# First attention of a two-block kernel: the last chunk's scores are computed a second time and its penalty is subtracted in PSUM

## The reference

```python
scores = jnp.einsum('bthd,bghd->bhtg', Q, K) / np.sqrt(DH)
topv, topi = jax.lax.top_k(scores, K_TOP)          # K_TOP = 32
probs = jax.nn.softmax(topv, axis=-1)
attn = jnp.zeros_like(scores).at[bi, hi, ti, topi].set(probs)
attn_mean = attn.mean(axis=1)                      # over the 4 heads
c_t = jnp.einsum('btg,bgd->btd', attn_mean, V)
```

## Time and profile before

| What | Value |
|---|---|
| Median of 3 executions | 2037.97 us (2029.82 to 2042.62) |
| Profiled execution, its own time | 2042.3 us |
| Its span in the trace | 2040.5 us |
| Mean granted TensorE clock | 0.889 of full speed |
| PE busy | 1603.4 us (79%) |
| ACT busy | 1387.9 us (68%) |
| DVE busy | 914.9 us (45%) |
| POOL busy | 180.9 us (9%) |
| L753 (scores, 832 passes) | 387.5 us |
| L907 (masking products, 128) | 239.3 us |
| L835 (exponentials, 128) | 208.9 us |
| L819 (copies of scores, 224) | 205.8 us |

### The profile page before, as it was taken

How to read it: one execution, slowest core, us unless ns; L and a number is a source line. 1 busy time by engine, 2 the same in 40 slices (tenths; PEclk the granted TensorE clock), 3 DMA queues, 4 the chain that set the end, 5 groups by cost and what they waited for, 6 DMA issues and landing times. The chain is left out here.

```text
span 2040.5 us, 23175 instructions
## 1 busy us (share of the span) xinstructions
PE 1603.4 (79%) x8229; PEld 618.9 (30%) x8229; DVE 914.9 (45%) x2862; ACT 1387.9 (68%) x1382; POOL 180.9 (9%) x153
## 2 busy tenths in 40 slices
PE   5347877879788878358351999999999999996996
PEld 3236334445445445244220111111111111113332
DVE  4733799999999999837131000000000000003323
ACT  3462767777778686520221999999999999993332
POOL 2753010111111111100000000000000000000000
PEclk7566978999998999679665999999999999997998
DMA  2122076776966967747302000430070000003000
GB/s 85 49 90 96 10 154 136 173 174 136 204 148 134 216 135 172 164 113 97 59 3 46 1 1 1 34 35 1 1 64 5 1 1 1 1 1 89 0 0 11
DMA packets 91353, 145.12 MB, mean 71 GB/s; under 512 B 46704, under 2 KB 59465, under 8 KB 90433
## 3 DMA queue, kind: packets, MB, share of 16 engines
q0 software_dynamic: 13472, 75.53, 18.7%
q1 hardware_dynamic: 77328, 67.19, 15.5%
q10 hardware_dynamic: 432, 0.85, 0.1%
HBM read 54.15 MB, written 13.99 MB: 33 GB/s over the span
## 5 line engine op out<-in xcount | busy, mean ns | idle before, releaser
L1735 ACT ACTIVATE ex<-ps 128x1536 f32<-128x1536 f32 x544 | 731.2, 1496 | 1.6 <-PE ps L1694 1.5
L1707 PE MATMUL ps<-ex,V 128*9 128x512 f32 x3264 | 427.6, 596 | 0.2 <-ACT ex L1735 0.2
L753 PE MATMUL ps<-K,qst 128*128 128x512 f32 (+1 forms) x832 | 387.5, 611 | 23.2 <-ACT srow L819 17.4
L1694 PE MATMUL ps<-Q,K 52*128 52x512 bf16 x1632 | 329.2, 385 | 67.5 <-PEq L106 33.7
L947 DVE MAX8 cand<-srow 128x8 f32<-128x128 f32 x1600 | 353.6, 283 | 6.9 <-ACT srow L819 6.5
L1745 DVE COPY o<-ps 9x512 f32<-9x512 f32 x32 | 22.0, 687 | 745.8 <-PE ps L1707 745.0
L819 ACT COPY srow<-ps 128x1024 f32<-128x1024 f32 (+1 forms) x224 | 205.8, 921 | 88.9 <-PE ps L753 88.1
L907 DVE SCALAR_TENSOR_TENSOR both<-srow,top,both 128x1536 f32<-128x1536 f32 (+1 forms) x128 | 239.3, 1870 | 13.1 <-ACT both L835 13.0
L753 PEld LDWEIGHTS ps<-K,qst 128*128 128x128 f32 x832 | 161.3, 205 | 182.2 <-issue 139.7
L835 ACT ACTIVATE both<-srow,shift 128x1536 f32<-128x1536 f32 (+1 forms) x128 | 208.9, 1635 | 7.7 <-DMA both<-both 6.6
L1694 PEld LDWEIGHTS ps<-Q,K 52*128 52x128 bf16 x1632 | 60.3, 94 | 484.8 <-ACT ex L1735 446.7
(11 more groups left out here) (306 smaller groups left out, 1142.2 us busy)
## 6 DMA issues: line engine op xcount, KB each, us to landing
both<-both POOLq DMA_DIRECT2D x69, 768.0 KB, 8.4
v_ring<-v_rows SPq DMA_DIRECT2D x96, 256.0 KB, 3.8
both<-both POOLq DMA_DIRECT2D x23, 898.0 KB, 12.5
K<-k_parts SPq DMA_DIRECT2D x48, 204.0 KB
k_parts<-kl SPq DMA_DIRECT2D x12, 384.0 KB, 2.5
V<-v_rows SPq DMA_DIRECT2D x4, 918.0 KB, 33.3
v_rows<-v1g SPq DMA_DIRECT2D x12, 288.0 KB, 3.0
v_rows<-V SPq DMA_DIRECT2D x12, 256.0 KB, 3.2
```

The source lines that it names most:

```text
L753: last = M.matmul(ps[:, GBANK * (k % RING) + b, 0:c1 - c0], qst[:, h, :], K0[:, c0:c1], start=True, stop=True)
L1694: last = M.matmul(ps[:, n % 6, :], K1[rows_, quad % 2, hh // 2, g * P:(g + 1) * P], Q1[rows_, 4 * quad + hh, tb * TB:(tb + 1) * TB], start ...
L1707: last = M.matmul(ps[32 * j:32 * j + VW, 6 + w % 2, :], V1[:, quad % 2, g, VW * j:VW * j + VW], ex1[:, (4 * g + j) % NSLOT, :], start=g == ...
L1735: C.activation(ex1[:, n % NSLOT:n % NSLOT + NBANK, :], ps[:, n % 6:n % 6 + NBANK, :], ACT.Exp)\
```

## The change

For items 0 to 30 the last chunk (columns 4608 to 6404) goes another way. ScalarE computes `penalty` = Relu(2^100 x (32nd largest - score)) in bf16 from `srow`: zero where the score is kept, very large elsewhere. TensorE computes the chunk's scores a second time into two more ring places (1024 and 772 columns, `AGAIN`) and adds to each, in the same PSUM accumulation, a bf16 product of `minus` (the negated identity) and `penalty`. ScalarE takes the exponential straight from that PSUM (`exps_again`), which gives zero where the penalty is large. VectorE's masking product of that chunk is gone; it computes one more column, `steep` = 2^100 x 32nd largest. The ring's places get a common numbering (`RING_AT`), the queries are placed two items ahead rather than four, VectorE's three other masks move to pieces 41, 45 and 49, and GpSimd's transfer for the last chunk of item n - 1 is issued ahead of those of item n. The last item, 31, is treated as before.

```diff
@@ -658,11 +658,21 @@
     CH_OF = [3, 3, 3, 4]
     NCH = len(CH_OF)
     CUTS = [min(4 * P * sum(CH_OF[:c]), G) for c in range(NCH + 1)]
+    LOW = NCH - 1
     LAST = NI - 1
     SLOTS = 3
-
-
-    MASK_AFTER = {38: 0, 42: 1, 46: 2, 49: 3}
+    STEEP = 2.0 ** 100
+
+
+    MASK_AFTER = {41: 0, 45: 1, 49: 2}
+    AGAIN = [(c0, min(c0 + GCOL, G)) for c0 in range(CUTS[LOW], G, GCOL)]
+    RING_AT = {}
+    for n in range(NI + 1):
+        for g in range(NGRP):
+            if n < NI:
+                RING_AT["first", n, g] = len(RING_AT)
+            if n >= 2 and g >= NGRP - len(AGAIN):
+                RING_AT["again", n - 2, g - NGRP + len(AGAIN)] = len(RING_AT)
     NEEDS = {j: c for c in range(NCH) for j in range(sum(CH_OF[:c]), sum(CH_OF[:c + 1]))}
     TURNED_BY = {c: sum(CH_OF[:c + 1]) for c in range(NCH)}
     SPREAD = [3, 5, 7, 9, 11, 13, 15, 17, 19, 21, 23, 24, 25]
@@ -687,6 +697,9 @@
         cand = sb(b2, "cand", [P, 2, LONG])
         top40 = sb(b2, "top40", [P, SLOTS, 40])
         edges = sb(b2, "edges", [P, NI, 3])
+        penalty = sb(b2, "penalty", [P, G - CUTS[LOW]], BF16)
+        minus = sb(b2, "minus", [P, P], BF16)
+        steep = sb(b2, "steep", [P, SLOTS])
         nmax = sb(b2, "nmax", [P, SLOTS])
         zsum = sb(b2, "zsum", [P, SLOTS])
         lnz = sb(b2, "lnz", [P, SLOTS])
@@ -719,7 +732,13 @@
             return (t * (H0 - 1) + h) * 16 * PARTS[c]

         def kept_by(n, c):
-            return n * NCH + c + 1
+            return n * LOW + c + 1
+
+        def evac_by(n, g):
+            return RING_AT["first", n, g] + 1
+
+        def again_by(n, r):
+            return RING_AT["again", n, r] + 1

         STEPS = 10

@@ -743,7 +762,7 @@
             def _(pe):
                 def scores(n, g):
                     t, h = divmod(n, H0)
-                    k = n * NGRP + g
+                    k = RING_AT["first", n, g]
                     if k >= RING:
                         pe.wait_ge(S("evac"), k - RING + 1)
                     pe.wait_ge(S("q_placed"), n + 1)
@@ -752,6 +771,19 @@
                         c0, c1 = g0 + b * 512, min(g0 + b * 512 + 512, g1)
                         last = M.matmul(ps[:, GBANK * (k % RING) + b, 0:c1 - c0], qst[:, h, :], K0[:, c0:c1],
                                         start=True, stop=True)
+                    last.then_inc(S("scored"), 1)
+
+                def scores_again(n, r):
+
+                    k = RING_AT["again", n, r]
+                    pe.wait_ge(S("evac"), k - RING + 1)
+                    pe.wait_ge(S("penalized"), n + 1)
+                    g0, g1 = AGAIN[r]
+                    for b in range(-(-(g1 - g0) // 512)):
+                        c0, c1 = g0 + b * 512, min(g0 + b * 512 + 512, g1)
+                        out = ps[:, GBANK * (k % RING) + b, 0:c1 - c0]
+                        M.matmul(out, qst[:, n % H0, :], K0[:, c0:c1], start=True, stop=False)
+                        last = M.matmul(out, minus[:, :], penalty[:, c0 - CUTS[LOW]:c1 - CUTS[LOW]], start=False, stop=True)
                     last.then_inc(S("scored"), 1)

                 def turn_group(u, j):
@@ -790,13 +822,18 @@
                         if j > 0:
                             value_group(u, j - 1)

-                for n in range(NI):
+                pe.wait_ge(S("minus_ready"), 1)
+                for n in range(NI + 1):
                     for g in range(NGRP):
-                        scores(n, g)
-                        mean_step(n * NGRP + g)
+                        if n < NI:
+                            scores(n, g)
+                        if ("again", n - 2, g - NGRP + len(AGAIN)) in RING_AT:
+                            scores_again(n - 2, g - NGRP + len(AGAIN))
+                        if n < NI:
+                            mean_step(n * NGRP + g)
                 if NI * NGRP - 1 in MEAN_AT:
                     value_group(*MEAN_AT[NI * NGRP - 1])
-                pe.wait_ge(S("evac"), NI * NGRP)
+                pe.wait_ge(S("evac"), len(RING_AT))
                 for j in range(NTURN):
                     turn_group(NT - 1, j)
                     if j > 0:
@@ -813,9 +850,12 @@
                     g0, g1 = group(g)
                     if n >= SLOTS:
                         below = [c for c in range(NCH) if CUTS[c] < g1]
-                        act.wait_ge(S("kept"), kept_by(n - SLOTS, below[-1]))
-                    act.wait_ge(S("scored"), n * NGRP + g + 1)
-                    b = GBANK * ((n * NGRP + g) % RING)
+                        act.wait_ge(S("kept"), kept_by(n - SLOTS, min(below[-1], LOW - 1)))
+                        if below[-1] == LOW:
+                            act.wait_ge(S("penalized"), n - SLOTS + 1)
+                    k = RING_AT["first", n, g]
+                    act.wait_ge(S("scored"), k + 1)
+                    b = GBANK * (k % RING)
                     C.copy(srow[:, n % SLOTS, g0:g1], ps[:, b:b + GBANK, :].rearrange("p a b -> p (a b)")[:, 0:g1 - g0])\
                         .then_inc(S("evac"), 1)

@@ -835,11 +875,28 @@
                     C.activation(both[:, home(n), chunk(c)], srow[:, s, chunk(c)], ACT.Exp, bias=shift[:, s:s + 1])\
                         .then_inc(S("exped"), 1)

+                def penalties(n):
+
+                    s = n % SLOTS
+                    act.wait_ge(S("steep_ready"), n + 1)
+                    C.activation(penalty[:, :], srow[:, s, chunk(LOW)], ACT.Relu, scale=-STEEP, bias=steep[:, s:s + 1])\
+                        .then_inc(S("penalized"), 1)
+
+                def exps_again(n, r):
+
+                    s, k = n % SLOTS, RING_AT["again", n, r]
+                    home_free(act, n, LOW)
+                    act.wait_ge(S("scored"), k + 1)
+                    b, (g0, g1) = GBANK * (k % RING), AGAIN[r]
+                    C.activation(both[:, home(n), g0:g1],
+                                 ps[:, b:b + GBANK, :].rearrange("p a b -> p (a b)")[:, 0:g1 - g0], ACT.Exp,
+                                 bias=shift[:, s:s + 1]).then_inc(S("evac"), 1)
+
                 def queries(n):

                     t, h = divmod(n, H0)
                     if t:
-                        act.wait_ge(S("scored"), (n - H0 + 1) * NGRP)
+                        act.wait_ge(S("scored"), again_by(n - H0, len(AGAIN) - 1))
                     rows_ = slice(DH0 * h, DH0 * (h + 1))
                     C.copy(qst[rows_, h, :], Q0[rows_, t * P:(t + 1) * P]).then_inc(S("q_placed"), 1)

@@ -864,6 +921,7 @@
                     C.copy(c_t[:, u, :], ps[:, 7, 0:D]).then_inc(S("c_read"), 1)

                 C.preload_act_table_set(BOTH_TABLE)
+                C.mul(minus[:, :], ident[:, :], -1.0).then_inc(S("minus_ready"), 1)
                 act.wait_ge(S("qst_zero"), 1)
                 for n in range(H0):
                     queries(n)
@@ -876,20 +934,21 @@
                         if older is not None:
                             if g == 2:
                                 exp_shift(older)
+                                penalties(older)
                                 exps(older, 0)
                             if g == 3:
                                 exps(older, 1)
                             if g == 4:
                                 exps(older, 2)
-                            if g == 5:
-                                exps(older, 3)
+                            if g >= NGRP - len(AGAIN):
+                                exps_again(older, g - NGRP + len(AGAIN))
                         if n < NI:
                             if k in MEAN_AT:
                                 mean_copy(*MEAN_AT[k])
                             if k in SUMS_AT:
                                 sums_copy(SUMS_AT[k])
-                    if n + H0 < NI:
-                        queries(n + H0)
+                    if n >= 2 and n + 2 < NI:
+                        queries(n + 2)
                 sums_copy(NT - 2)
                 exp_shift(LAST)
                 for c in range(NCH):
@@ -935,12 +994,15 @@
                         if r == 0:
                             V.tensor_scalar(nmax[:, s:s + 1], top40[:, s, 0:1], -1.0, None, ALU.mult)\
                                 .then_inc(S("nmax_ready"), 1)
+                        if r == 3:
+                            V.tensor_scalar(steep[:, s:s + 1], top40[:, s, TOPK - 1:TOPK], STEEP, None, ALU.mult)\
+                                .then_inc(S("steep_ready"), 1)

                 def maxes(n, p):

                     g = p * PIECE // GCOL
                     if p * PIECE == g * GCOL:
-                        dve.wait_ge(S("evac"), n * NGRP + g + 1)
+                        dve.wait_ge(S("evac"), evac_by(n, g))
                     c0 = p * PIECE
                     c1 = G if G - c0 < 2 * PIECE else c0 + PIECE
                     eight = cand[:, n % 2, FEW:LONG].rearrange("p (r q) -> p r q", q=NPIECE)[:, :, p]
@@ -991,7 +1053,10 @@
                     t, h = divmod(n, H0)
                     if h == 0:
```

(12 more changed lines are left out.)

## The result

The changed kernel takes 2072.47 us (median of 4, 2067.47 to 2073.68) against 2036.68 before (median of 4, 2029.82 to 2042.62): ratio 1.0161, 95% interval 1.0136 to 1.0186. That is 35.8 us slower, where 2060 (+22) had been forecast within 2010 to 2090. The profiled execution took 2071.96 us, its span is 2070.1 us.

A forecast was written before the change was run, and what follows sets the result against it. VectorE was taken to bound the kernel at 19.97 us per item, with TensorE binding after the change. Terms +22.3, -9.4, +6.0 and clock +4 gave +23 on 2042.3: 2065, or 2060 on the median, range 2010 to 2090.

The forecast's parts named there:

- VectorE: Per item, the masking product's 1.99 us goes and about 0.1 is added, leaving VectorE alone needing 18.1 us.
- TensorE's work: Per item, 3.0 us of repeated scores and 0.75 of bf16 passes raise TensorE from 15.0 to 18.8 us.
- ScalarE: Per item, penalties of 1.70 us and a split exponential raise ScalarE from 14.6 to 16.5 us, below both others.
- The waits: TensorE waiting for ScalarE's copies, laid out for four kinds of item by mean-step places: 2.1 us per item.
- TensorE binds but its waits close: Rival: TensorE runs further ahead, items cost 18.8 to 19.6 us, total 2016, range 2005 to 2035; chance 0.23.
- The sum: Item costs over the whole stage: together +19 us, +23 with the clock, giving 2060 on the median.
- the 23 items beside regular steps: VectorE items alongside regular mean steps: 0.97 us more each, +22.3 in all.
- the four early items: Items without mean steps at the stage's start, run at VectorE's 18.1 us: 1.9 us less each.
- the two hurried items: Stage end, 13 mean steps in 14 groups: from 43.2 us with a regular one before to 49.2, +6.0.
- The clock: TensorE's slow stretches at 1.2 GHz become rarer but every one is now paid: +4 us in all.
- the fourth kind: Items with mean steps at 21, 23, 24, 25: a 3.0 us wait for a mean copy, 22.35 us long.
- the third kind: Items with mean steps at 15, 17, 19: laid out like the first kind, 19.87 us long.

The follow-up runs named there:

- experiment 4: Changed kernel with a useless VectorE reduction over 1796 columns per item in place of the removed product: 2074.84 us, ratio 1.0167.
- the eleventh: Changed kernel without the second fp32 scores and with the full penalty for item 0 only: 2003.02 us, ratio 0.9839.
- experiment 1: Changed kernel without the four bf16 products of minus and penalty per item: 2053.98 us, ratio 1.0085.
- experiment 3: Changed kernel with ScalarE computing the full penalty for item 0 only, 8 columns of it afterwards: 2035.80 us, ratio 0.9981.
- Experiment 2: Changed kernel without the second computation of the last chunk's scores, bf16 penalty product kept: 2055.51 us, ratio 1.0074.
- the seventh: Changed kernel with shift and penalties in group 1, mean copy before the exponential (groups 2 to 4), 1284 columns computed twice: 2030.11 us.
- the ninth: Kernel before the change, with ScalarE's copy of the mean made ahead of the exponential in groups 2 to 4: 2045.78 us, ratio 1.0038.

## Why the prediction was right, step by step

- *VectorE.* Right: freed by 1.9 us per item, and off the path (experiment 4). Its bound of 18.1 us is seen in the eleventh at 18.03.
- *TensorE's work.* Right: 0.21 us per bf16 pass, nothing for the weights in between. The 18.8 us bound in sum, with the waits; taking the penalty's 0.75 us away gave 0.6 per item back (experiment 1).
- *ScalarE.* Right in size (1.792 us) and in place: of the work added, taking off the penalties gave back most (experiment 3, -36.7 us; moved ahead of copy 2, -18.4). The forecast gave them 1.1 us of wait per item; experiment 3 has 42.7 / 31 = 1.4 for the 1.5 us taken off, with what the clock gave back in it. The Trainium skill (ScalarE: Activation LUTs, Rules for kernel authors) advises VectorE for relu. No run here shows what that would give, since none tried it there. What the runs show is why it hurt on ScalarE: the instruction stood between two copies for which TensorE waits.
- *The waits.* The kinds of wait are those laid out, and two of the four kinds of item repeat within 0.11 us of the layout; the third does in two of six, the fourth in none. The rival "TensorE binds but its waits close" failed: they did not close by themselves, only with another order and less work.
- *The sum.* Direction and range were right, the size too small: +22 forecast, +35.8 measured. In the stage of the profiles it is +41.7 against a sum of +19 without the clock and +23 with it. By its terms: the 23 items beside regular steps cost +37.2 (500.5 us, 463.3 before) where +22.3 was summed; the four early items won 3.8 (picks 243.99 to 320.05 against 245.98 to 325.86), not 7.5; the two hurried items with the last cost 72.4 us against 63.1, +9.3 where +6.0 - 1.9 was summed, and there the 2 us of waits were 2.96 and 2.83. (The first interval is 0.9 shorter.) That the profiled execution still came near its 2065 (2071.96) is luck: the unchanged code was 14.7 us shorter in it than in the profile before.
- *The clock* is the term that was most mis-sized: +4 in all. The grant rose from 0.92 to 0.97, as its working had it, but the slow stretches that were left were paid for. Of the six items of the fourth kind, laid out at 22.35 us, one had the full clock and took 23.38; five had 0.93 and took 24.10, 25.30, 24.79, 24.26 and 24.72. Of the third kind, two with long waits for value blocks took 20.48 and 20.54 at 1.00, two took 22.89 and 22.29 at 0.93 and 0.92. Of the four early ones two took 18.0 and 18.1, two 19.8 and 20.1 (granted 0.92 and 0.94). From these differences I estimate 5 x 1.25 + 2 x 2.1 + 3.7 = 14 us for the clock ahead of the hurried items (the waits for value blocks, which differ by up to 0.8 us within a kind, are in it). No run held the clock apart from the waits, so this is read from the traces and not shown by an experiment. Experiment 2 shows the other side: 0.93 with less work, and little gained.
- *What the layout left out* is the value blocks. The item of the fourth kind at the full clock (23.38 against 22.35) has a wait of 0.55 us for one; the rest of its excess is open. All four items of the third kind above 20 us have one, of 1.73 to 2.48 us.

## What to carry to other kernels

Before work is moved off the engine that sets the pace, lay out one period of the others in order, with their waits for each other, and not only their sums: here ScalarE's sum had room, but the new instruction stood in the one place where TensorE's ring had run out. Put added work where its engine waits anyway, and move only as much as levels the engines: 772 columns instead of 1796, with the penalty in the earlier group and a third value buffer, gave 1998.33 us, 1.9% under the kernel before. And a wait that costs nothing still shields others: when it goes, see what comes late next. Last, once an engine binds, price its stretches at the lower clock in full: of the six items of the fourth kind the five at 0.93 took 0.7 to 1.9 us more than the one at the full clock.

## What the runs showed that was not expected

- TensorE's waits for value blocks: 4.9 us before, 11.3 after, 27.8 in the seventh and 33.4 in the ninth, with the same loads and two buffers in each. The trace after shows single loads that take very long. SyncE issued one at 431.19 us, as its buffer came free, and TensorE could start on it at 441.53 only, after 1.73 us of waiting: 10.3 us, with the steps two groups apart. From issue to landing these loads took 4.0 us at the median and 11.0 at the longest (before 4.0 and 10.5). What makes some so long was not settled.
- The lower clock did not follow every wait of the same length. Without mean steps TensorE waited 1.67 us in each early item: behind the waits that end at 260.74 and 298.71 it ran slower, behind the one that ends at 280.57 it did not. In the fourth kind, behind the wait of 2.96 us, it did in five items of six.
- TensorE with 94 us less work (experiment 2) finished its stage only 25 us sooner, at a clock of 0.93 instead of 0.97.
- A section of unchanged code, from the inverse transform's first pass to the next matmul stage, took 52.9 to 68.2 us in the fourteen profiles, a spread as large as many of the effects under study; the stage's own length leaves it out.
